# Graph layer on one core: the step from the edge pass to the node update

## The reference, cut to what matters

```python
xn = _layernorm(x)
# message passing, edges sorted by dst
gate = sigmoid(silu(rbf @ W1 + b1) @ W2 + b2)          # 50000 x 256
aggr = segment_sum(gate * xn[src], dst)
upd = silu(concat([xn, aggr]) @ U1 + c1) @ U2 + c2
gnn = xn + upd
# attention without softmax: one 256x256 matrix for all nodes
mix = (q @ (k.T @ v / S)) @ wo.T + bo
x = x + gnn + mix
x = x + experts(_layernorm(x))                          # top 2 of 16
```

## Time and profile before

| | us |
|---|---|
| median of 3 runs | 1153.02 (1151.21 to 1155.04) |
| the profiled execution | 1151.01 |
| its span, first to last instruction | 1149.2 |
| TensorE busy | 1050.9 (91%) |
| VectorE busy | 896.5 (78%) |
| GpSimd busy | 761.7 (66%) |
| ScalarE busy | 670.3 (58%) |
| mean granted TensorE clock | 0.957 of full speed |

### The profile page before, as it was taken

How to read it: one execution, slowest core, us unless ns; L and a number is a source line. 1 busy time by engine, 2 the same in 40 slices (tenths; PEclk the granted TensorE clock), 3 DMA queues, 4 the chain that set the end, 5 groups by cost and what they waited for, 6 DMA issues and landing times.

```text
span 1149.2 us, 23535 instructions
## 1 busy us (share of the span) xinstructions
PE 1050.9 (91%) x7924; PEld 990.9 (86%) x7924; DVE 896.5 (78%) x1331; ACT 670.3 (58%) x1023; POOL 761.7 (66%) x720
## 2 busy tenths in 40 slices
PE   4897999999999999999999989983499999999992
PEld 2466899999999999999999889972499999999992
DVE  7877998888898888889988815858667777777770
ACT  2562766666666666666667434430067767677761
POOL 5457777777777777777777746401456777767752
PEclk9998999999999999999999979975899999999996
DMA  8211444454544444544444301222168888889864
GB/s 240 71 52 51 142 143 140 141 143 143 145 142 141 140 141 142 145 144 141 142 140 142 84 3 60 92 88 80 67 180 235 238 229 232 226 227 237 235 137 131
DMA packets 115689, 165.14 MB, mean 144 GB/s; under 512 B 15394, under 2 KB 88151, under 8 KB 115543
## 3 DMA queue, kind: packets, MB, share of 16 engines
q1 hardware_dynamic: 83942, 95.11, 26.0%
q0 software_dynamic: 31104, 68.19, 24.5%
q10 hardware_dynamic: 560, 0.79, 0.2%
HBM read 145.55 MB, written 21.68 MB: 146 GB/s over the span
## 4 chain that ended last, share of the span: by engine, by line
PE 85%; DVE 8%; issue 3%; ACT 1%; DMA 1%; PEld 1%; POOL 0%; DVEq 0%; POOLq 0%; ACTq 0%; PEldq 0%; SPq 0%
PE ps L1426 24%; PE ps L1595 16%; PE ps L1437 15%; PE ps L1607 8%; PE ps L1380 8%; PE ps L1482 3%; PE ps L1354 2%; PE ps L1499 2%; PE ps L1490 2%; PE ps L1582 1%; PE ps L1513 1%; PE ps L1363 1%; PE ps L1347 1%; PE ps L1364 1%; DVE st L917 1%
## 5 line engine op out<-in xcount | busy, mean ns | idle before, releaser
L1426 PE MATMUL ps<-fr 128*128 128x256 f32 x2352 | 306.9, 287 | 3.2 <-DVE fr L979 3.2
L1426 PEld LDWEIGHTS ps<-fr 128*128 128x128 f32 x2352 | 289.4, 192 | 4.1 <-DVE fr L979 4.1
L565 POOL DMA_INDIRECT big<-xn_rows,srcs x200 | 218.7, 1094 | 60.8 <-issue 60.8
L565 POOL DMA_INDIRECT hgx<-xn_rows,srcs x192 | 210.6, 1097 | 58.5 <-issue 58.5
L718 ACT ACTIVATE h1f<-ps,b 128x512 f32<-128x512 f32 x196 | 124.0, 684 | 165.6 <-PE ps L1380 164.4
L1437 PEld LDWEIGHTS ps<-oh,big 128*128 128x128 f32 x1568 | 192.9, 194 | 10.8 <-issue 2.8
L1595 PE MATMUL ps<-fr 128*128 128x256 f32 x1536 | 192.5, 285 | 2.7 <-issue 1.4
L1437 PE MATMUL ps<-oh,big 128*128 128x96 f32 x1568 | 191.2, 276 | 2.6 <-DVE big L1115 2.6
L1595 PEld LDWEIGHTS ps<-fr 128*128 128x128 f32 x1536 | 189.0, 194 | 3.3 <-issue 1.8
L979 DVE TENSOR_TENSOR fr<-h1f,fr 128x1024 fp32r<-128x1024 f32 x98 | 120.1, 1225 | 52.7 <-ACT fr L721 52.6
L1292 DVE TENSOR_TENSOR fr<-big,fr 128x1024 fp32r<-128x1024 f32 x96 | 117.4, 1223 | 30.3 <-ACT fr L831 29.9
(11 more groups left out here) (190 smaller groups left out, 1387.6 us busy)
## 6 DMA issues: line engine op xcount, KB each, us to landing
big<-in_w SPq DMA_DIRECT2D x128, 256.0 KB, 4.2
rbf<-in_rbf SPq DMA_DIRECT2D x98, 256.0 KB, 2.9
big<-in_w SPq DMA_DIRECT2D x32, 512.0 KB, 4.0
xn_rows<-xn SPq DMA_DIRECT2D x38, 128.0 KB, 1.7
big<-xn_rows,srcs POOLq DMA_INDIRECT x200, 3.1
out<-out_rows SPq DMA_DIRECT2D x1, 3125.0 KB, 11.7
hgx<-xn_rows,srcs POOLq DMA_INDIRECT x192, 3.2
out_rows<-x_nodes SPq DMA_DIRECT2D x3, 768.0 KB, 3.7
```

Source lines behind the costliest of these rows:

```text
L565: pool.indirect_dma_start(hg[i % HB][:, s, :], None, xn_d[:, :], bass.IndirectOffsetOnAxis(srcs[:, col:col + 1], 0))\
L1426: last = mm(ps[:, 2 + 4 * p + s // 2, (s % 2) * D:(s % 2 + 1) * D], h1s[p][a][:, c, s * P:(s + 1) * P], W2s[b][:, c, :], start=c == 0 and ...
```

## The change

The change has four parts.

- The low parts of `U1` (in two halves), `U2` and `M` are no longer subtracted by GpSimd after its last gather. VectorE subtracts them in the edge pass, one after each of the groups of four tiles 6 to 9 (`update_low`), in instructions of 128x512. ScalarE casts the high parts after the pairs 6, 7 and 8 instead of beside the last ones, and waits for `s_mv` (M is complete) first.
- TensorE gives `s_uo` and `s_ux` at the very start of its program. ScalarE casts xn of the first two pairs (`node_high(0, 0)`, `node_high(1, 1)`, first part each) before it waits for `s_gnn`. GpSimd makes the low parts in the order xn 0, xn 1, aggregate 0, aggregate 1; those of xn are counted by the new `s_nxl`.
- VectorE gives `s_x1` before `s_gnn`; the copy of one element is gone and a wait for its own count of `add_window` stands in its place.
- TensorE no longer waits for `s_gnn` itself. It waits for the four low parts, for the first xn low, makes the `M` products of the first pair, then the first 6 `U1` products, and waits for the aggregate's low part (`s_nlo`) only there. From the second pair on the order is as before.

```diff
@@ gpsimd
             edges(0)
-            pool.wait_ge(s_uhi, 3)
-            low(U1s, U1[:, :, :])
-            low([u[:, 0:DC, :] for u in UMs], U2[:, :, :])
-            low([u[:, DC:2 * DC, :] for u in UMs], M).then_inc(s_ulo, 1)
             pool.wait_ge(s_flag, 1)
...
-            node_low(0, 0)
-            node_low(1, 1)
+            for k in range(2):
+                for q in range(2):
+                    pool.wait_ge(s_nhi, 2 * k + q + 1)
+                    low((xns, ags)[k][q], (xnT, agg)[k][:, :, q * 2 * P:(q + 1) * 2 * P])\
+                        .then_inc((s_nxl, s_nlo)[k], 1)
             silu_low(0, 0)
@@ scalar
-                steps(act, n0, 0, NG // 2 - 6, pair)
-                for j in range(NG // 2 - 6, NG // 2 - 2):
+                def pair_cast(j):
                     pair(j)
-                    if type(n0) is int and j < NG // 2 - 3:
+                    if type(n0) is int and 6 <= j < 9:
+                        act.wait_ge(s_mv, 3)
                         dst, src = ((U1s[0], U1[:, :, :]), (UMs[0][:, 0:DC, :], U2[:, :, :]),
-                                    (UMs[0][:, DC:2 * DC, :], M))[j - NG // 2 + 6]
+                                    (UMs[0][:, DC:2 * DC, :], M))[j - 6]
                         act.copy(dst, src).then_inc(s_uhi, 1)
+                steps(act, n0, 0, NG // 2 - 2, pair_cast)
...
             node_high(0, 0, parts=(0,))
+            node_high(1, 1, parts=(0,))
             act.wait_ge(s_gnn, 1)
             node_high(0, 0, parts=(1,))
-            node_high(1, 1)
+            node_high(1, 1, parts=(1,))
             u1_silu(0, 0)
@@ vector
+            def update_low(k):
+
+                dve.wait_ge(s_uhi, (1, 1, 2, 3)[k])
+                halves, of = (([u[:, 0:DC, :] for u in U1s], U1[:, 0:DC, :]),
+                              ([u[:, DC:2 * DC, :] for u in U1s], U1[:, DC:2 * DC, :]),
+                              ([u[:, 0:DC, :] for u in UMs], U2[:, :, :]),
+                              ([u[:, DC:2 * DC, :] for u in UMs], M))[k]
+                dve.tensor_tensor(halves[1], of, halves[0].bitcast(f32), ALU.subtract).then_inc(s_ulo, 1)
...
-                steps(dve, n0, 0, (NG - 6) // HB, four)
+                def four_low(j):
+                    four(j)
+                    if type(n0) is int and 6 <= j < 10:
+                        update_low(j - 6)
+                steps(dve, n0, 0, (NG - 6) // HB, four_low)
...
-            link(dve.tensor_copy(v_a[:, 0:1], agg[:, 0, 0:1]))
+            dve.sem_inc(s_x1, 2)
+            dve.wait_ge(s_agg, NG + 2)
             dve.sem_inc(s_gnn, 1)
...
-            dve.sem_inc(s_x1, 2)
@@ tensor
+            pe.sem_inc(s_uo, 2)
+            pe.sem_inc(s_ux, 2)
             pe.wait_ge(s_const, 1)
...
-            pe.sem_inc(s_uo, 2)
-            pe.sem_inc(s_ux, 2)
-            pe.wait_ge(s_gnn, 1)
-            pe.wait_ge(s_ulo, 1)
-            def node_xn(v, q, n=2):
-                pe.wait_ge(s_nlo, v + 1)
+            pe.wait_ge(s_ulo, 4)
+            def node_u1(v, q, first=False):
+                if not first:
+                    pe.wait_ge(s_nlo, v + 1)
                 pe.wait_ge(s_us, v + 1)
-
                 for m in range(DC):
                     for k in range(2 * DC):
+                        if first and m == 0 and k == DC:
+                            pe.wait_ge(s_nlo, v + 1)
                         for a, b in PARTS:
...
+
+            def node_m(v, q, n=2):
                 pe.wait_ge(s_x1, v + 1)
...
+            def node_xn(v, q, n=2):
+                node_u1(v, q)
+                node_m(v, q, n)
...
-            node_xn(0, 0)
+            pe.wait_ge(s_nxl, 1)
+            node_m(0, 0)
+            node_u1(0, 0, first=True)
```

More of the change, by code:

```diff
@@ L317, in gps_layer @@
         s_nlo = sem("node_operands_low")
+        s_nxl = sem("first_xn_low")
         s_ux = sem("xn_parts_done")
```

## The result

| | before | after |
|---|---|---|
| median of 8 runs each, us | 1151.12 (1149.31 to 1155.04) | 1145.99 (1144.28 to 1147.54) |
| profiled execution | 1151.01 | 1145.69 |
| span | 1149.2 | 1143.9 |
| TensorE / VectorE / ScalarE / GpSimd busy | 1050.9 / 896.5 / 670.3 / 761.7 | 1046.2 / 895.5 / 670.5 / 757.6 |
| mean granted clock | 0.957 | 0.961 |

The ratio is 0.9949, 95% interval 0.9939 to 0.9959: 5.1 us less, where 10.85 were forecast. The way was right and the size twice too large.

A forecast was written before the change was run, and what follows sets the result against it. TensorE's pace bounds the edge pass; at its end TensorE stands idle and its clock falls. Gap at 658 2.7 + scatter clock 2.8 + handover 2.7 + first pair's clock 2.65 = 10.85 us less: 1142.2 us, range 1139 to 1147.5.

The forecast's parts named there:

- Tail without the held one-hot: End of edge pass: no held one-hot, last scatter over at 662.2 not 667.68; 5.5 us, 2.7 gap and 2.8 clock.
- Subtractions in mid pass at no cost: Mid edge pass: four VectorE subtractions of 0.69 us fit in its slack; cost nothing, 2.8 us if none were covered.
- Rival D: Mid edge pass: the four subtractions stall TensorE; takes back 2.8 us, or 13.6 with clock falls, 1155.8; chance 0.07.
- Handover: Last scatter to first node product: `s_x1` comes last, gap 1.4 us in place of 4.1; 2.7 us less.
- Clock over the first pair: Node products of the first pair: clock stays at 1.00, 36 products take 4.35 us instead of 7.0; gain 2.65.
- B: Rival at the handover: the clock falls all the same amid thin scatter products; 1145.3 us, chance 0.11.
- E: Rival at the node update's start: `s_x1` or aggregate's low part as late as before; 1147.5 us, chance with C 0.08.
- C: Rival in the tail: GpSimd's early xn low parts hold message 97 and delay scatter 97; 1147.5 us, chance with E 0.08.

The follow-up runs named there:

- short block: The changed kernel with TensorE's never-entered block for left-over edges cut to a single wait; ratio 0.9915 to the kernel before, step 164.7 us.
- each of the two main parts alone: Kernel before with only VectorE's mid-pass low parts: ratio 0.9958; changed kernel with those subtractions back on GpSimd, keeping early counts and new order: 0.9972.
- the node update written twice: The changed kernel with TensorE's node update once ahead of the jump and once inside the left-over block; ratio 0.9947 to the kernel before, step 164.9 us.

## Why the prediction came out as it did

The figures of the first four points compare the first profile of each side, as the prediction did; the point on the sum gives the means of three.

- **Tail without the held one-hot, 5.5 us:** right. From the last first-layer product to the last scatter product 20.8 became 15.5 us, 5.3 less, with no gap at 658, the clock at 1.00 and the last scatter over within 0.3 us of where the sum put it (663.5, less the 1.1 by which the pass was later).
- **Subtractions in mid pass at no cost:** right. They took 0.68 to 0.69 us at 289.8 to 356.8, and TensorE was busy 80.00 of 80 us between 280 and 360. From the first gate product to the last first-layer product the pass took 540.7 us, and 539.3, 540.7 and 540.3 in the three profiles before. Rival D is out.
- **Handover, 2.7 us: the step that failed.** The prediction said that TensorE needs three counts and that "`s_x1` is the last". The count did come 1.4 us after the last scatter. But TensorE's stream was inside its jump for another 1.4 us: 0.9 us were gained (4.12 to 3.22), not 2.7. I had put down TensorE's late count in the earlier trace rows to "TensorE's own read of the flag", with 0.88 us, and measured it from the end of the products. The stream begins the read at about the time that the last scatter starts, 3.9 us before its products are over in that profile (663.8, 667.68), 1.9 us in the changed kernel (661.6, 663.5), and slow scatter products hid most of the jump. Taking the slow products away laid the jump bare.
- **Clock over the first pair, 2.65 us:** mis-sized as a consequence. It was 0.50 again, behind a gap of 3.22 us instead of 1.4. The 36 products took 5.7 us (666.74 to 672.45), not 4.35; 1.3 us gained. With the gap at 1.5 us (short block) the clock stayed and they took 4.4. So B's symptom was there, but not by B's cause, the thin scatter products around a short gap.
- **E** is the rival that came true in the trace (first product more than 2.5 us behind the last scatter), by another mechanism than the late counts that it named. **C** did not happen in the changed kernel: message 97 (659.89) was 1.1 us ahead of GpSimd (660.97). Moving TensorE's scatter by 1.6 us was enough to make it happen.
- **The sum:** 5.3 + 0.9 + 1.3 = 7.5 us, where the steps of the two first profiles differ by 7.7 and the means of three on each side by 7.2 (175.4, 168.2). By the means the parts are others: 4.5 in the tail (20.1, 15.6), 2.2 in the gap (5.4, 3.2) and 0.5 in the 36 products (6.5, 6.1; they took 7.0, 5.8 and 6.9 us before). The end of the handover failed in all three profiles of the changed kernel, 3.1 to 3.3 us instead of 1.4, and with it the clock. How much of the 10.85 each term owes to the kernel before depends on the profile that is read, and the prediction had one. With the jump gone (short block) the parts are 4.5, 3.9 and 2.2, together 10.6.
- **Alone and together:** each of the two main parts alone brings 4.0 us, which would make 8.0, and together they bring 7.2. The 0.8 us between is less than three profiles of one kernel differ by, so it isn't shown whether the parts add.
- **The range:** the measured 1145.99 lies in the 1139 to 1147.5, near B's 1145.3, and luck has a share in that. Forecast and range were laid from a median of 1153.02 of three runs, 2.0 above the profiled one; over eight runs it is 1151.12. The same 10.85 and the same widths laid from there give 1140.3 and 1137.1 to 1145.6, and 1145.99 is just outside.
- **Left open:** 7.2 us in the step, 5.1 in the medians, whose interval reaches to 7.0. The first profile before had its pass 1.0 to 1.5 us shorter than the two later ones, whose spans, 1151.5 and 1151.3, are 7.5 us above the changed kernel's 1143.9. Whether the timed executions of before had shorter steps than its profiled ones, no run here shows.

The Trainium skill has the rule that I missed (Runtime: NRT & Kernel Launch, Instruction fetch mechanics): a taken branch whose target lies outside the pages of code already loaded makes the engine fetch the target's page before it goes on. The page gives no price. The traces agree with it in kind: 3.33 to 3.94 us in each of the 12 profiles of kernels with the large block, 0.23 with a block of one wait, 0.08 to 0.10 for a branch not taken. That it is the fetch of code, and not some other cost of a far jump, is the page's word; the runs show only that a large block costs this and a block of one wait doesn't. No size between was run, and the branches of VectorE, ScalarE and GpSimd over their own blocks for left-over edges are recorded with 0.05 to 0.07 us; whether that is the engine or the block, no run here separates.

## What to carry to other kernels

Take more than one profile of the kernel as it stands before you price a term: three of this one had the same step within 1.7 us, but the gap at the handover was 4.1 us in one and 5.9 and 6.3 in the others. A stage's last stall can hide the ones beneath it: before you take it away, look up what each engine's instruction stream does in the same microseconds (flag reads, branches), since the busy view doesn't show it. In this kernel TensorE's jump over a large block that is never entered costs it some 3.5 us, so put it where that engine waits for another one anyway, and let the common case fall through, if need be by writing it twice. Work of GpSimd on SBUF beside VectorE's two-input instructions belongs where VectorE has slack, and is to be checked again whenever the order around it moves by a microsecond.

## What was not expected of the hardware

A gap of the same length can cost the clock or not. Ahead of the first-layer products at 126 us TensorE stood 2.23 us in the first profile before and the clock stayed at 1.00. In the changed kernel it stood 2.25 us at the same place, and the clock fell:

```profile
125.76 1.19 PE L1397 MATMUL ps<-fr 128*128 128x512 f32 x4 [2.25 <-DVE fr L976]
```

```profile
127.00:128.00 1.00, 1.00 (x8) 1.00 (x6) 1.00 (x2) 1.00 (x2) 0.79 (x1) 0.52 0.98 344
128.00:129.00 1.00, 1.00 (x6) 1.00 (x6) 1.00 (x2) 0.91 (x2) 0.91 (x1) 0.50 0.48 150
```

The pass of the changed kernel is 1.4 us longer than that of the kernel before in the two first profiles. This is not the change's doing: in the second and third profiles before, unaltered, the gap there is 2.24 and 2.23 us, the clock falls behind it too, and the pass is 1.5 and 1.0 us longer than in the first. The same pair of profiles has it once more, ahead of the gate products of tile 97: a gap of 2.23 us in both, then 0.50 and 4.40 us for the 24 products in the second profile (above), 1.00 and 3.13 us in the third:

```profile
656.24 3.13 PE L1426 MATMUL ps<-fr 128*128 128x256 f32 x24 [2.23 <-DVE fr L979]
```

At the handover a gap of 0.42 us, and one of 1.52 us in the kernels with a short block and with the node update written twice, left the clock at 1.00. It was at 0.50 behind every gap of 2.83 to 6.25 us.
